# Four batches' attention weights per group: two turned by 32x32 block transposes and quadrant moves, two by TensorE

## The chip, the cores and the metric

The kernel runs on one core of one Trainium2 chip. The metric is device time in microseconds (us) of one execution. Engines are called PE (TensorE; PEld is its weight load), DVE (VectorE), ACT (ScalarE), POOL (GpSimd) and SP (the engine that issues the DMAs here).

## The reference, cut to what matters

A stack of four graph layers on x of shape (32 batches, 256 nodes, 128 features), each followed by `layernorm(x + layer(x))`: a gated graph layer, a two-layer graph network with batch norm over all 32 batches, a graph attention, and two graph convolutions followed by LSTMs over windows of 1 to 4 nodes. The change lies in the attention:

```python
Wh = jnp.einsum('bnf,fo->bno', h, W)
e = s1[:, :, None] + s2[:, None, :]
e = jnp.where(e >= 0, e, ALPHA * e)
e = jnp.where(adj_matrix[None] == 0, -jnp.inf, e)
attention = jax.nn.softmax(e, axis=-1)
h_prime = jnp.einsum('bij,bjo->bio', attention, Wh)
```

A product on PE contracts over partitions. The exponentials are made with node i on the partitions, and the mix over j needs them with j there: each batch's 256x256 matrix has to be turned, as four squares of 128x128.

## The kernel before, in words

The 32 batches are worked on in 8 groups of four (`GB = 4`). The first two layers run over all groups, because the batch norm needs all of them. Then come slots, s = 2 to 10: slot s does the attention of group s (part A, s up to 7), the graph convolutions of group s-1 (B), the LSTM of group s-2 (L) and the last norm of group s-3 (T). Groups 0 and 1 have their attention ahead of the slots. Every engine has its own program, written out by hand in `slot(...)`; engines meet by semaphores. So slots 2 to 7 do the work that the change touches, and slots 3 to 7 hold all four parts.

The LSTM has 11 steps k = 0 to 10 (`STEPS`; windows of 3 nodes are steps 4 to 6, windows of 4 are steps 7 to 10). A step is: on PE the products with x (`lstm_x`, L855, written x(k)) and with the state before (`lstm_h`, L867, written h(k)), on ACT the gates (L1231), on DVE the cell (`inner(k)`: L1712, L1718, L1722), on ACT its tanh (L1267), on DVE the state (`state(k)`, L1740), which h(k+1) waits for through `h_ok`. x(7) also waits for state(6), since the windows of 4 read what the windows of 3 have written.

The attention of a group in its slot: DVE adds the mask and takes the maximum into `MS` (`a_max`), ACT makes leaky ReLU (`a_lin`, L1184) and exponential (`a_exps`, L1194) into `E1`; PE turns each batch by four transposes into a PSUM bank (`a_turn_e`, L770), DVE copies the bank into `MS` (`a_weights`, L1640, 512 columns); PE mixes (`a_mix`, L791), ACT copies the result (L1172), PE projects it (L801), DVE adds it (L1664). The banks are `AB[0..3]`: the first half of PB, the first of PA, the second of PB, the second of PA. `a_hidden` (L1700, DVE) reads PA into the state buffer of the LSTM's next group and ends with `h1_ok`; the odd batches' bank is in PA and so waits for it.

`MS` and `E1` are the parts k = 0 and 1 of `late`, 2048 columns each. POOL does the reciprocal roots of the norms (L450), the norms' outputs (`scale2`, L518, into X1, and `tail`, L531, into the output buffer). SP only stores outputs during the slots (L425). The order on PE near the change is

```python
x(7)
x(8)
a_turn_e(s, range(GB)) if A else None
h(8)
x(9)
if A:
    a_mix(s, (0, 1, 2))
    a_project_mix(s, (0, 1))
h(9)
```

Of the kernel before, what the change touches and what calls it, by code (L numbers as in the profile page):

```python
# [100 lines left out]
def build(nc, x, xt, adj, early_in, later_in, lstm_w, out):  # L101
    ctx = ExitStack()
    with ctx:
# [20 lines left out]
        ZF = late[:, 3, 2 * BANK:4 * BANK]  # L124

# [126 lines left out]
        copied_ok = sem("copied_ok")  # L252
# [144 lines left out]
        def _(sp):  # L397
# [25 lines left out]
            for g in range(GROUPS - 1):  # L423
                sp.wait_ge(ln[3]["out"], TILES * (g + 1))
                sp.dma_start(out[g], OUT[:, g % 2]).then_inc(sent[g % 2], 16)  # L425
# [11 lines left out]
        def _(pool):  # L437
# [125 lines left out]
        def _(pe):  # L563
# [192 lines left out]
            def a_turn_e(g, some):  # L756
                f = front(g)
                for b in some:
                    if b % 2 == 0:
# [6 lines left out]
                    pe.wait_ge(exps_ok, GB * g + b + 1)  # L766
                    for c in range(NC):
                        for m in range(NC):
                            at = m * NODES + c * P
                            mm = pe.transpose(f.AB[b][:, at:at + P], f.E1[:, 2 * b + c, m * P:(m + 1) * P], ident[:])  # L770
                    mm.then_inc(et_ps, 1)
# [13 lines left out]
            def a_mix(g, some):  # L785
                pe.wait_ge(ln[1]["out"], TILES * (g + 1))
                f = front(g)
                for b in some:
                    pe.wait_ge(pt_ok, GB * (g - 1) + b + 1)
                    for m in range(NC):  # L790
                        mm = pe.matmul(f.AB[b][:, 0:NODES], turned(X2, m, b), f.MS[:, 2 * b + m, :],  # L791
# [127 lines left out]
            def slot(s, par, A, B, L, T):  # L919
# [69 lines left out]
                a_turn_e(s, range(GB)) if A else None  # L989
# [69 lines left out]
        def _(act):  # L1059
# [209 lines left out]
            def slot(s, par, A, B, L, T):  # L1269
# [102 lines left out]
        def _(dve):  # L1372
# [457 lines left out]
            def slot(s, par, A, B, L, T):  # L1830
# [48 lines left out]
                cell(6)  # L1879
                a_hidden(s - 1, 1 - par) if B else None  # L1880
# [105 lines left out]
```

## Time and profile before

| what | before |
|---|---|
| median of 3 runs | 635.05 us (634.25 to 636.53) |
| the profiled execution: its own time | 635.21 us |
| its span in the trace | 633.4 us |
| busy share PE / PEld / DVE / ACT / POOL | 98% / 68% / 74% / 69% / 26% |
| a slot with all four parts | 57.5 us |

The span is what the trace covers; the 1.8 us between it and the execution's own time lie around the program. A group of equal instructions in the timeline has one line: start, length, engine, line of code, operation, output and input, how many, and in brackets the idle time ahead of it with what ended it. For products in float32 the trace has two records each, for transposes one.

### The profile page before, as it was taken

The page shows a single profiled execution, that of the slowest core. Times are in us where ns is not written, and L with a number is a line of the kernel's source. Part 1 is how long each engine was busy: PE and PEld are TensorE (multiplying, and loading weights), DVE is VectorE, ACT ScalarE, POOL GpSimd, SP SyncE. Part 2 cuts the span into 40 slices and gives each one's busy share as a digit, 9 for nine tenths or more (in the row PEclk, how much of TensorE's full clock was granted, in tenths as well). Part 3 has the DMA queues.
Part 4 walks back from the last instruction along what each step waited for, and adds up shares of the span by engine and source line. Part 5 has one row for each costly group of instructions (what it writes and reads, how often), then busy time and mean ns, then how long its engine had stood idle before and what let it go on. Part 6 is the DMA issues. An engine that isn't in the chain of part 4 may idle for free.

```text
span 633.4 us, 9530 instructions
## 1 busy us (share of the span) xinstructions
PE 617.9 (98%) x2738; PEld 433.9 (68%) x2738; DVE 470.4 (74%) x1623; ACT 435.6 (69%) x1000; POOL 167.3 (26%) x228
## 2 busy tenths in 40 slices
PE   9999999999999999999999999999999999999994
PEld 6645556448975686578568757865885686577794
DVE  3999999877847658866887787688769867365656
ACT  3678786957847765784777678567857766546774
POOL 1465541005332003204403240340143032103201
PEclk9999999999999999999999999999999999999998
DMA  8334000000000000000000000000000000000000
GB/s 331 136 130 167 1 2 0 0 1 2 1 1 1 1 2 0 2 1 34 2 1 1 33 2 1 35 2 1 1 33 2 0 35 1 1 0 35 1 35 35
DMA packets 4372, 16.85 MB, mean 27 GB/s; under 512 B 480, under 2 KB 480, under 8 KB 4192
## 3 DMA queue, kind: packets, MB, share of 16 engines
q1 hardware_dynamic: 4320, 16.25, 6.7%
q8 instruction: 22, 0.36, 0.2%
q14 instruction: 30, 0.25, 0.1%
HBM read 12.05 MB, written 4.19 MB: 26 GB/s over the span
## 4 chain that ended last, share of the span: by engine, by line
PE 77%; DVE 3%; ACT 3%; issue 2%; POOL 1%; ACTq 0%; POOLq 0%; DVEq 0%
PE QQ L855 26%; PE QQ L867 15%; PE PA L838 4%; PE PA L810 4%; PE PB L829 2%; PE PB L820 2%; PE PB L691 2%; PE PA L691 2%; PE PA L791 2%; PE PB L791 2%; PE PA L644 1%; PE QQ L889 1%; PE PB L908 1%; PE PB L770 1%; PE PA L770 1%
## 5 line engine op out<-in xcount | busy, mean ns | idle before, releaser
L1231 ACT ACTIVATE raw<-QQ,BL 128x256 f32<-128x256 f32 (+2 forms) x279 | 150.1, 558 | 75.1 <-PE QQ L867 37.7
L855 PE MATMUL QQ<-HT,WT 128*128 128x256 f32 (+2 forms) x558 | 183.9, 474 | 1.1 <-ACT raw L1231 0.6
L450 POOL TENSOR_TENSOR RSD<-VAR,pw 128x4 f32<-128x4 f32 (+1 forms) x43 | 61.8, 1438 | 376.2 <-DVE VAR L1454 376.2
L855 PEld LDWEIGHTS QQ<-HT,WT 128*128 128x128 f32 x558 | 103.5, 190 | 59.3 <-issue 28.3
L867 PE MATMUL QQ<-HB,WT 128*128 128x256 f32 (+2 forms) x336 | 100.2, 441 | 0.4 <-DVE HB L1740 0.2
L867 PEld LDWEIGHTS QQ<-HB,WT 128*128 128x128 f32 x336 | 61.2, 190 | 29.3 <-issue 13.4
L1267 ACT ACTIVATE raw<-raw 128x256 f32<-128x256 f32 (+4 forms) x79 | 37.1, 470 | 25.9 <-DVE raw L1722 19.7
L1712 DVE SCALAR_TENSOR_TENSOR raw<-raw 128x256 f32<-128x256 f32 (+2 forms) x60 | 32.5, 542 | 20.2 <-ACT raw L1231 19.6
L1740 DVE SCALAR_TENSOR_TENSOR HB<-raw 128x256 f32<-128x256 f32 (+4 forms) x42 | 20.1, 478 | 23.5 <-ACT raw L1267 23.5
L1066 ACT ACTIVATE X<-Z,OFF,RSD 128x128 f32<-128x128 f32 x80 | 31.8, 481 | 2.5 <-POOL OFF L456 2.5
L518 POOL TENSOR_SCALAR X<-four,MEAN,RSD 128x128 f32<-128x128 f32 x64 | 30.7, 494 | 1.6
L1194 ACT ACTIVATE HB<-HB,EB 128x256 f32<-128x256 f32 x64 | 30.9, 501 | 0.2
L644 PE MATMUL PA<-AHT,X 128*128 128x256 f32 x128 | 29.6, 384 | 1.3 <-ACT X L1066 1.3
L810 PE MATMUL PA<-AD,X 128*128 128x256 f32 x128 | 30.3, 379 | 0.0
L531 POOL TENSOR_SCALAR four<-HB,MEAN,RSD 128x128 f32<-128x128 f32 x56 | 29.6, 543 | 0.7
L658 PE MATMUL QQ<-one_b,later 128*128 128x512 f32 x64 | 29.1, 597 | 0.6 <-ACT one_b L1100 0.6
L838 PE MATMUL PA<-AD,Y 128*128 128x256 f32 x128 | 29.2, 380 | 0.0
L644 PEld LDWEIGHTS PA<-AHT,X 128*128 128x128 f32 x128 | 23.7, 190 | 7.7 <-issue 4.8
L810 PEld LDWEIGHTS PA<-AD,X 128*128 128x128 f32 x128 | 23.8, 191 | 6.8 <-issue 4.1
L838 PEld LDWEIGHTS PA<-AD,Y 128*128 128x128 f32 x128 | 24.2, 190 | 4.3
L621 PE MATMUL PB<-four,AD 128*128 128x512 f32 x56 | 26.2, 611 | 0.0
L1112 ACT ACTIVATE HB<-QQ 128x512 f32<-128x512 f32 x32 | 18.0, 587 | 11.5 <-PE QQ L658 10.1
(254 smaller groups left out, 1164.5 us busy)
## 6 DMA issues: line engine op xcount, KB each, us to landing
four<-in_x SPq DMA_DIRECT2D x8, 512.0 KB, 4.0
raw<-in_xt SPq DMA_DIRECT2D x8, 512.0 KB, 6.6
out<-four SPq DMA_DIRECT2D x7, 512.0 KB, 2.7
WT<-in_lstm SPq DMA_DIRECT2D x1, 2048.0 KB, 9.3
later<-in_later SPq DMA_DIRECT2D x1, 725.5 KB, 10.2
AD<-in_adj SPq DMA_DIRECT2D x2, 256.0 KB, 4.8
out<-four SPq DMA_DIRECT2D x2, 256.0 KB, 2.0
early<-in_early SPq DMA_DIRECT2D x1, 289.0 KB, 4.7
```

The source lines that it names most:

```text
L450: pool.tensor_tensor(RSD[kk][:, ts], VAR[kk][:, ts], pw[:, ts], ALU.pow).then_inc(ln[k]["rstd"], some)
L518: pool.tensor_scalar(tile_of(X1, g, c, b), nth(f.Z2, t), MEAN[f.kk2][:, t:t + 1], RSD[f.kk2][:, t:t + 1], ALU.add, ALU.mult).then_inc(ln[2 ...
L644: mm = pe.matmul(PA[:, b * NODES:(b + 1) * NODES], tile_of(X1, g, m, b), AHT[:, m, :], start=(m == 0), stop=(m == NC - 1))
L810: mm = pe.matmul(PA[:, b * NODES:(b + 1) * NODES], tile_of(X1, g, m, b), ADJT[:, m, :], start=(m == 0), stop=(m == NC - 1))
L838: mm = pe.matmul(PA[:, b * NODES:(b + 1) * NODES], turned(Y, m, b), ADJT[:, m, :], start=(m == 0), stop=(m == NC - 1))
L855: mm = pe.matmul(steps_view(Q[q], k), WT[:, 0, (p - 1) * 4 + q, :], ht_view(par, k), start=True, stop=(s == 0))
L867: pe.matmul(Q[q][:, 0:nw * GB], WT[:, 1, (p - 1) * 4 + q, :], HS[:, (k - 1) % 2, 0:nw * GB], start=False, stop=True).then_inc(g_ps, 1)
L1066: act.activation(nth(to, t), nth(z, t), ACT.Identity, bias=OFF[kk][:, t:t + 1], scale=RSD[kk][:, t:t + 1]).then_inc(ln[k]["out"], 1)
L1194: e = act.activation(f.E1[:, t], f.E1[:, t], ACT.Exp, bias=f.EB[:, t:t + 1], scale=1.0, accum_out=DEN[:, t:t + 1] if g > 1 else None)
L1231: act.activation(TG[q][:, at:n], Q[q][:, at:n], ACT.Tanh, scale=0.5 if q == G else 0.25, bias=BL[:, p - 1, q:q + 1]).then_inc(g_ok, 1)
L1267: act.activation(TC[:, at:n], CELL[:, at:n], ACT.Tanh, scale=0.5).then_inc(tc_ok, 1)
L1712: dve.scalar_tensor_tensor(out=target[:, 0:n], in0=TG[I][:, 0:n], scalar=1.0, in1=TG[G][:, 0:n], op0=ALU.add, op1=ALU.mult).then_inc(cell_ ...
```

## The change

In slots 2 to 7 (groups g of 2 and more):

- Batches 0 and 1 are no longer turned by PE. DVE transposes every 32x32 block of a batch in place of its quadrant (`a_turn_blocks`, one instruction of 512 columns per batch, `E1` to `MS`); the blocks then stand in the right order within 32 partitions but in the wrong quadrant of 32 partitions. Sixteen moves of 32 partitions by 256 columns, for both batches at once, bring them from `MS` back to `E1`: eight by DMAs from SP (`move_blocks`), eight by copies of POOL (`carry_blocks`), each of which waits until the one before is complete, the four that stay in their quadrant among them.
- Batches 2 and 3 are turned by PE into the first and the second half of PB, and copied to `MS` as before. They wait for `y1_ok` alone, not for `h1_ok`.
- `a_mix` of batches 0 and 1 reads the moved blocks, with an access of 2x4 runs of 32 columns; it waits for all moves. Odd batches wait for `h1_ok` there, even ones for the copies that free PB.
- `a_hidden` goes behind the copy of batch 2; DVE's block transposes stand ahead of and behind `inner(6)`; ACT makes the exponentials of batch 1 one place earlier and those of batch 2 one place later.
- On POOL the eight copies stand ahead of `tail`; on SP the eight DMAs of slot s stand ahead of the store of group s-3.

```diff
+            def move_blocks(g, h):
+                sp.wait_ge(tr_ok, 2 * (g - 1))
+                for q, c in DMA_BLOCKS:
+                    sp.dma_start(block_at(1, h, c, q), block_at(0, h, q, c)).then_inc(moved_ok, 16)
...
+            def carry_blocks(g, h):
+                pool.wait_ge(tr_ok, 2 * (g - 1))
+                pool.wait_ge(yt_ok, upto(g + 3))
+                n = len(POOL_BLOCKS) * (g - 2)
+                for k, (q, c) in enumerate(POOL_BLOCKS):
+                    reach(pool, carried_ok, n + k)
+                    pool.tensor_copy(block_at(1, h, c, q), block_at(0, h, q, c)).then_inc(carried_ok, 1)
+                pool.wait_ge(carried_ok, n + len(POOL_BLOCKS))
...
-                    pe.wait_ge(pt_ok, GB * (g - 1) + b + 1)
+                    if b < 2:
+                        pe.wait_ge(moved_ok, 16 * len(DMA_BLOCKS) * (g - 1))
+                        pe.wait_ge(carried_ok, len(POOL_BLOCKS) * (g - 1))
+                    else:
+                        pe.wait_ge(pt_ok, GB + 2 * (g - 2) + b - 1)
+                    if b % 2:
+                        reach(pe, h1_ok, 2 * g)
+                    else:
+                        pe.wait_ge(pt_ok, GB + 2 * (g - 2) + b // 2 + 1)
...
-                a_turn_e(s, range(GB)) if A else None
+                a_turn_e(s, (2, 3)) if A else None
...
+            def a_turn_blocks(g, some):
+                for b in some:
+                    dve.wait_ge(exps_ok, GB * g + b + 1)
+                    dve.wait_ge(lin_ok, GB * g + 2)
+                    dve.transpose(by_block(0, b // 2)[:, :, b % 2].rearrange("p q c m i -> p (c m) q i"),
+                                  E1[:, 2 * b:2 * b + 2].rearrange("p c (m q i) -> p (c m) q i", m=NC, q=4)).then_inc(tr_ok, 1)
...
-                cell(6)
-                a_hidden(s - 1, 1 - par) if B else None
+                a_turn_blocks(s, (0,)) if A else None
+                inner(6)
+                a_turn_blocks(s, (1,)) if A else None
+                state(6)
+                a_hidden(s - 1, 1 - par) if B and not A else None
...
-                a_weights(s, (0, 1)) if A else None
+                if A:
+                    a_weights(s, (2,))
+                    a_hidden(s - 1, 1 - par)
+                    a_weights(s, (3,))
                 cell(8)
                 if A:
-                    a_weights(s, (2, 3))
                     a_inverse(s)
```

The order on DVE in a slot, from x(7)'s predecessor to the cell of step 8. L1693 is a_biased1, L1712 to L1740 the LSTM's cell and state, L1700 a_hidden, L1640 the copy out of a PSUM bank. Before:

```order
L1693 TENSOR_TENSOR Y<-PB,later 128x1024
L1712 SCALAR_TENSOR_TENSOR raw<-raw 128x340
L1718 SCALAR_TENSOR_TENSOR raw<-raw 128x340
L1722 SCALAR_TENSOR_TENSOR raw<-raw 128x340
L1740 SCALAR_TENSOR_TENSOR HT<-raw 128x85x4
L1700 TENSOR_SCALAR HT<-PA 128x4x256
...
L1712 SCALAR_TENSOR_TENSOR raw<-raw 128x256
L1740 SCALAR_TENSOR_TENSOR HB<-raw 128x256
L1640 COPY HB<-PB 128x512
L1640 COPY HB<-PA 128x512
```

The same place in the change; L1754 is now a_biased1, L1693 the block transpose, L1773 to L1801 cell and state, L1701 the copy, L1761 a_hidden:

```order
L1754 TENSOR_TENSOR Y<-PB,later 128x1024
L1693 STREAM_TRANSPOSE HB<-HB 128x4x4x32
L1773 SCALAR_TENSOR_TENSOR raw<-raw 128x340
L1779 SCALAR_TENSOR_TENSOR raw<-raw 128x340
L1783 SCALAR_TENSOR_TENSOR raw<-raw 128x340
L1693 STREAM_TRANSPOSE HB<-HB 128x4x4x32
L1801 SCALAR_TENSOR_TENSOR HT<-raw 128x85x4
...
L1773 SCALAR_TENSOR_TENSOR raw<-raw 128x256
L1801 SCALAR_TENSOR_TENSOR HB<-raw 128x256
L1701 COPY HB<-PB 128x512
L1761 TENSOR_SCALAR HT<-PA 128x4x256
L1701 COPY HB<-PB 128x512
```

Two transposes came in ahead of state(6), a_hidden went from there to behind state(7), and two of four copies are gone.

On POOL in the same slot, the change only (L552 are the eight copies, L474 and L565 the tail, L542 scale2); before, L450 and L531 stood where L474 and L565 stand, with nothing ahead of them:

```order
L534 TENSOR_SCALAR HB<-HB,BN 128x1024
L552 COPY HB<-HB 32x256 x8
L474 TENSOR_TENSOR RSD<-VAR,pw 128x8
L565 TENSOR_SCALAR four<-HB,MEAN,RSD 128x128 x8
L474 TENSOR_TENSOR RSD<-VAR,pw 128x4
L542 TENSOR_SCALAR X<-four,MEAN,RSD 128x128 x4
```

## Rows read from the trace of the kernel before

**Rows 1.** The page: engine, busy us (share of the span), instructions.

```profile
PE 617.9 (98%) x2738; PEld 433.9 (68%) x2738; DVE 470.4 (74%) x1623; ACT 435.6 (69%) x1000; POOL 167.3 (26%) x228
```

**Rows 2.** Windows, second and last of six slots: stretch, its length, busy us (instructions).

```profile
core 0: us, PE busy (x) PEld busy (x) DVE busy (x) ACT busy (x) POOL busy (x), PEclk, DMA share, GB/s
...
223.63:281.14 57.51, 57.51 (x252) 41.44 (x250) 43.34 (x148) 40.27 (x91) 9.74 (x13) 1.00 0.00 1
...
453.64:511.14 57.50, 57.50 (x251) 41.44 (x250) 43.70 (x154) 40.39 (x91) 14.52 (x21) 1.00 0.03 10
```

**Rows 3.** Timeline of PE from x(7) of a slot on: start us, length us.

```profile
453.64 3.19 PE L855 MATMUL QQ<-HT,WT 128*128 128x256 f32 x14
456.67 0.60 PE L770 MATMUL PB<-ident,HB 128*128 128x128 f32 x4
...
458.41 1.89 PE L867 MATMUL QQ<-HB,WT 128*128 128x256 f32 x8
460.14 1.89 PE L855 MATMUL QQ<-HT,WT 128*128 128x256 f32 x8
461.87 1.03 PE L791 MATMUL PB<-HB,X 128*128 128x256 f32 x4
```

**Rows 4.** Timeline of PE's weight loads in the same stretch.

```profile
453.43 3.00 PEld L855 LDWEIGHTS QQ<-HT,WT 128*128 128x128 f32 x14
...
458.30 1.60 PEld L867 LDWEIGHTS QQ<-HB,WT 128*128 128x128 f32 x8
...
461.65 0.84 PEld L791 LDWEIGHTS PB<-HB,X 128*128 128x128 f32 x4
...
465.24 1.60 PEld L867 LDWEIGHTS QQ<-HB,WT 128*128 128x128 f32 x8
```

**Rows 5.** Timeline of DVE in the same slot, idle time ahead in brackets.

```profile
448.16 1.23 DVE L1693 TENSOR_TENSOR Y<-PB,later 128x1024 f32<-128x1024 f32 x1
449.82 0.51 DVE L1712 SCALAR_TENSOR_TENSOR raw<-raw 128x340 f32<-128x340 f32 x1 [0.44 <-ACT raw L1231]
...
452.21 0.51 DVE L1740 SCALAR_TENSOR_TENSOR HT<-raw 128x340 f32<-128x340 f32 x1 [0.68 <-ACT raw L1267]
453.90 2.02 DVE L1700 TENSOR_SCALAR HT<-PA 128x1024 f32<-128x1024 f32 x1 [1.18 <-PE PA L838]
...
457.48 0.43 DVE L1740 SCALAR_TENSOR_TENSOR HB<-raw 128x256 f32<-128x256 f32 x1 [0.55 <-ACT raw L1267]
457.82 0.68 DVE L1640 COPY HB<-PB 128x512 f32<-128x512 f32 x1
...
459.98 0.54 DVE L1712 SCALAR_TENSOR_TENSOR raw<-raw 128x256 f32<-128x256 f32 x1 [0.89 <-ACT raw L1231]
...
461.94 0.47 DVE L1740 SCALAR_TENSOR_TENSOR HB<-raw 128x256 f32<-128x256 f32 x1 [0.55 <-ACT raw L1267]
```

**Rows 6.** Timeline of DVE in slot 2, whose x(7) starts at 223.63.

```profile
225.75 0.42 DVE L1712 SCALAR_TENSOR_TENSOR raw<-raw 128x256 f32<-128x256 f32 x1
226.99 0.42 DVE L1740 SCALAR_TENSOR_TENSOR HB<-raw 128x256 f32<-128x256 f32 x1 [0.82 <-ACT raw L1267]
```

**Rows 7.** Timeline of POOL in the slot of rows 3, and one wait for itself.

```profile
428.70 0.20 POOL L456 TENSOR_TENSOR OFF<-MEAN,RSD 128x8 f32<-128x8 f32 x1 [0.17 <-POOL RSD L450]
456.67 1.75 POOL L450 TENSOR_TENSOR RSD<-VAR,pw 128x8 f32<-128x8 f32 x1 [27.77 <-DVE VAR L1454]
458.52 4.21 POOL L531 TENSOR_SCALAR four<-HB,MEAN,RSD 128x128 f32<-128x128 f32 x8
471.02 1.01 POOL L450 TENSOR_TENSOR RSD<-VAR,pw 128x4 f32<-128x4 f32 x1 [8.29 <-DVE VAR L1454]
```

**Rows 8.** Groups of POOL by shape: busy us, mean ns of one.

```profile
L518 POOL TENSOR_SCALAR X<-four,MEAN,RSD 128x128 f32<-128x128 f32 x64 | 30.7, 494 | 1.6
...
L510 POOL TENSOR_SCALAR HB<-HB,BN 128x1024 f32<-128x1024 f32 x7 | 8.6, 1239 | 1.2 <-DVE HB L1578 1.2
```

**Rows 9.** SP's issues at the start of the program: start us, length us.

```profile
1.15 0.42 SPq L402 DMA_DIRECT2D four<-in_x  x1
1.62 0.42 SPq L406 DMA_DIRECT2D early<-in_early  x1
```

**Rows 10.** The page's DMA issues: count, KB each, median us from issue to landing.

```profile
raw<-in_xt SPq DMA_DIRECT2D x8, 512.0 KB, 6.6
...
out<-four SPq DMA_DIRECT2D x2, 256.0 KB, 2.0
```

More of the change, by code:

```diff
@@ L124, in build, with by_block, block_at @@
         ZF = late[:, 3, 2 * BANK:4 * BANK]
+        def by_block(k, h):
+            return late[:, k, h * COLS:(h + 1) * COLS].rearrange("p (q b c m i) -> p q b c m i", q=4, b=2, c=NC, m=NC)
+        def block_at(k, h, quadrant, slot):
+            at = h * COLS + slot * NODES
+            return late[32 * quadrant:32 * quadrant + 32, k, at:at + NODES]
+        DMA_BLOCKS = [(q, (q + n) % 4) for n in (1, 2) for q in range(4)]
+        POOL_BLOCKS = [(q, (q + n) % 4) for n in (0, 3) for q in range(4)]
         AN = late[:, 0, 0:BANK].rearrange("p (c n) -> p c n", c=NC)
@@ L251, in build @@
                              "turned_ok"))
-        copied_ok = sem("copied_ok")
+        copied_ok, tr_ok = sem("copied_ok"), sem("tr_ok")
+        moved_ok = sem("moved_ok")
+        carried_ok = sem("carried_ok")
         f_half, cf_half, cell_half, tc_half = (sem(n) for n in ("f_half", "cf_half", "cell_half", "tc_half"))
@@ L421, in _ @@
             sp.dma_start(WT[:], lstm_w).then_inc(lstm_in, 16)
-            for g in range(GROUPS - 1):
-                sp.wait_ge(ln[3]["out"], TILES * (g + 1))
-                sp.dma_start(out[g], OUT[:, g % 2]).then_inc(sent[g % 2], 16)
+            def move_blocks(g, h):
+                sp.wait_ge(tr_ok, 2 * (g - 1))
+                for q, c in DMA_BLOCKS:
+                    sp.dma_start(block_at(1, h, c, q), block_at(0, h, q, c)).then_inc(moved_ok, 16)
+            for s in range(2, GROUPS + 2):
+                if s < GROUPS:
+                    move_blocks(s, 0)
+                if s >= 3:
+                    g = s - 3
+                    sp.wait_ge(ln[3]["out"], TILES * (g + 1))
+                    sp.dma_start(out[g], OUT[:, g % 2]).then_inc(sent[g % 2], 16)
             half = TILES // 2 * P
@@ L537, in slot @@
                     scaled(s + 2)
+                if A:
+                    carry_blocks(s, 0)
                 if T:
@@ L758, in a_turn_e @@
                 for b in some:
-                    if b % 2 == 0:
+                    if g > 1:
+                        reach(pe, y1_ok, 2 * g)
+                    elif b % 2 == 0:
                         pe.wait_ge(max_ok, TILES * g + 4 * (b // 2 + 1))
@@ L766, in a_turn_e @@
                     pe.wait_ge(exps_ok, GB * g + b + 1)
+                    to = f.AB[b] if g < 2 else PB[:, b % 2 * BANK:(b % 2 + 1) * BANK]
                     for c in range(NC):
@@ L769, in a_turn_e @@
                             at = m * NODES + c * P
-                            mm = pe.transpose(f.AB[b][:, at:at + P], f.E1[:, 2 * b + c, m * P:(m + 1) * P], ident[:])
+                            mm = pe.transpose(to[:, at:at + P], f.E1[:, 2 * b + c, m * P:(m + 1) * P], ident[:])
                     mm.then_inc(et_ps, 1)
@@ L1179, in a_lin @@
                     act.wait_ge(max_ok, TILES * g + 2 * b + 2)
-                    reach(act, et_ps, GB * before(g))
+                    reach(act, et_ps, GB * before(g)) if g <= 2 else act.wait_ge(px_ps, GB * (g - 2))
                     for c in range(NC):
@@ L1303, in slot @@
                     a_lin(s, (1,))
-                    a_exps(s, (0,))
-                    a_lin(s, (2,))
+                    a_exps(s, (0, 1))
                 gates(6)
-                a_lin(s, (3,)) if A else None
+                a_lin(s, (2,)) if A else None
                 state(6)
-                a_exps(s, (1, 2)) if A else None
+                if A:
+                    a_lin(s, (3,))
+                    a_exps(s, (2,))
                 gates(7)
@@ L1638, in a_weights @@
                 for b in some:
-                    dve.wait_ge(et_ps, GB * g + b + 1)
-                    dve.tensor_copy(f.MS[:, 2 * b:2 * b + 2].rearrange("p m n -> p (m n)"), f.AB[b]).then_inc(pt_ok, 1)
+                    dve.wait_ge(et_ps, GB * g + b + 1 if g < 2 else GB * 2 + 2 * (g - 2) + b - 1)
+                    src = f.AB[b] if g < 2 else PB[:, b % 2 * BANK:(b % 2 + 1) * BANK]
+                    dve.tensor_copy(f.MS[:, 2 * b:2 * b + 2].rearrange("p m n -> p (m n)"), src).then_inc(pt_ok, 1)
             def a_sum2(g, some):
```

7 lines of the change are left out of this document (6 added, 1 removed).

## Prediction, on record before the changed kernel ran

> **What bounds the kernel now.** I read the busy times first [rows 1]: PE is busy for 98% of the span, DVE for 74%, ACT for 69%, POOL for 26%. The windows say it more sharply [rows 2]: cut from one slot's x(7) to the next one's, PE is busy for 57.51 of 57.51 us, and for 57.50 of 57.50 us in the last full slot. PE has no gap, so in these slots every microsecond taken from PE shortens the program, as long as nobody becomes late for PE. Nothing else can shorten it, so the gain cannot exceed the PE work removed. The timelines [rows 3 to 7] then tell how early each partner is.
>
> A PE product waits ahead of its weight load, so deadlines are read from the weight loads [rows 4]: x(7) at 453.43, h(8) at 458.30, the first mix at 461.65, h(9) at 465.24.
>
> **The change part by part.**
>
> *Transposes leave PE.* Between 456.67 and 458.41 the sixteen transposes of four batches run [rows 3]: 1.74 us, half of it 0.87 us per slot. Six slots (2 to 7) give 5.2 us. The mixes of batches 0 and 1 now stream eight runs of 32 columns instead of one of 256. I cost that at nothing: x(7) to x(10) already read the state buffer in runs of 4 columns, and x(9) takes exactly the 1.73 us (460.14 to 461.87) that h(8), which reads a contiguous buffer, takes (458.41 to 460.14) [rows 3].
>
> *DVE: two block transposes in, two copies out.* No row shows a block transpose. The nearest one is a one-input instruction over as many columns, the copy out of a bank, 0.68 us [rows 5], and I take that. Below lies the cell operation with 340 columns, 0.51; above, a_hidden, which writes strided and takes 2.02 us for 1024 columns, so 1.01 for 512 [rows 5]. The total on DVE is then unchanged; the place counts. The first transpose goes into the gap of 0.44 us ahead of inner(6), the second into the gap of 0.68 us ahead of state(6) [rows 5], where DVE waits for ACT. With T = 0.68 state(6) comes 0.24 + 0 = 0.24 us later. It ended at 452.72, and x(7)'s weights load at 453.43: a margin of 0.71, which covers it. The cover is gone when 2T - 1.12 = 0.71, at T = 0.92. At T = 1.01 PE waits 0.19 us per slot, 1.1 us in all.
>
> *h(8) is asked for 0.87 us earlier.* It waits for state(7), which ended at 457.91, while h(8)'s weights now want to load at 458.30 - 0.87 = 457.43. What helps is that a_hidden has left its place ahead of inner(7): in slot 2, where no last norm delays DVE and DVE is in time for ACT, state(7) starts at 226.99 and ends at 227.41 [rows 6], 3.78 us behind x(7). In the slot of rows 3 that is 457.42. ACT then sets the time (three exponential instructions' worth of work stand between the gates and the tanh, as before). 457.42 against 457.43 is no margin: with the semaphore's way and a weight load that no longer hides, I take 0.1 us of waiting per slot, 0.6 us in all. Lower end: 0. Upper end: POOL now works during this stretch, and beside POOL's tail DVE's cell operation took 0.54 instead of 0.42 us and its state 0.47 [rows 5, 6]; with that on both, 0.3 per slot, 1.8 us.
>
> *a_hidden moves behind state(7)* and one copy. From 457.5: copy to 458.1, a_hidden to 460.0, second copy to 460.6. Queued behind are inner(8) and state(8). The chain from inner(8) to the end of state(8) took from 459.98 to 462.41 [rows 5], so 2.43 us; it now ends at 463.0, and h(9)'s weights load at 465.24 - 0.87 = 464.37. Covered, with 1.3 us left. The odd mix that waits for `h1_ok` comes after 461.
>
> *The moves.* Both block transposes are done at about 451.5 + 0.24 + 0.68 = 452.4. The first mix's weights load at 461.65 - 0.87 = 460.8. So there are 8.4 us for the moves.
> SP: issues follow one another by 0.47 us [rows 9], the eighth starts 3.3 us after the first; landing 2.0 us for the smallest store, 6.6 us for the slowest kind of load [rows 10]. I take 2.0, since a move is 32 KB and touches no DRAM: done at 457.7. At 6.6 it would be 462.3, 1.5 us late.
> POOL: 128 columns take 0.49 us and 1024 take 1.24 [rows 8], so 0.84 ns per column more and 0.60 us for 256; the wait for its own result adds 0.17 [rows 7]. Eight in a row: 6.2 us, done at 458.6, 2.2 us early. Lower end: 0.49 each with no wait, 3.9 us. Upper end: 1.24 + 0.17 each, 11.3 us, done at 463.7.
> Behind the copies stands the tail, 1.75 + 4.21 us [rows 7]: done at 464.6; POOL's next work comes at 471.02 - 0.87. Covered. On SP only the store stands behind.
>
> *ACT* swaps exponentials of batches 1 and 2 between two places of equal length; nothing.
>
> **Sum.** 635.21 (the profiled execution) - 5.2 + 0.6 = 630.6. The median of the runs lies 0.16 below that execution, so 630.4 us.
>
> **Two rules of the Trainium skill.** Beside POOL's tail DVE's two-input cell operation lengthened by 0.12 us, from 0.42 to 0.54 [rows 5, 6]: a small brush, not a blockade. "SBUF — State Buffer", section "Who interferes with whom", says that a DVE instruction with two SBUF inputs and a POOL instruction that reads SBUF exclude each other for a whole instruction, and the loser fully blocks. By that rule the result would be rival B's; this trace agrees that there is an interaction but not with its size.
> The nearest row for a block transpose is 0.68 us. "VectorE: DVE Perf Modes", section "The three transpose paths", gives 311 ns for 128x128 in bf16; four of them would be 1.24 us (an estimate from that page), and the sum by it would be about 634; no row here shows it.
>
> **The rivals.**
>
> *A. The copies on POOL are late (slower).* Place: the wait of the first mix for `carried_ok`. If a copy that shifts quadrants costs as much as POOL's costliest one-input row, 1.24 + 0.17, the eight end at 463.7, 2.9 us behind 460.8; less the 0.87 saved this is 2.0 us per slot, 12 us: 647. It decides from (8.4 + 0.87)/8 = 1.16 us per copy on; from 1.05 on it eats into the gain. For it: only 32 of 128 partitions work, the copy leaves its quadrant, and nothing like it is in the trace. Against it: all elementwise rows of POOL lie below 0.6 us at this size. The DMAs at 6.6 us would do the same at a lower price (1.5 us late, 0.6 net per slot, 639).
>
> *B. The gain is given back on DVE (no change).* Two ways to the same time. A block transpose of twice the copy, 1.36 us, makes state(6) late by 2.72 - 1.12 - 0.71 = 0.89 us per slot, 5.3 us: 635. Or a copy of POOL (0.60) stands in the way of state(6) and of state(7) each once a slot: 0.24 + 0.60 - 0.71 = 0.13 and 0.1 + 0.60 = 0.7, together 0.8 per slot, with the 5.2 saved 634.8. For: both new partners of DVE are unseen. Against: the 0.12 us above.
>
> *C. Half a gain:* T between 0.9 and 1.2, or 0.3 to 0.5 us of waiting at h(8): 631.9 to 633.5.
>
> *D. The full gain,* nothing waits: 629.9. It lies within the forecast's own range.
>
> That the change doesn't do what it says I exclude: the order of instructions shows the transposes gone.
>
> **How the numbers follow.** Forecast with D: 0.66 (629.4 to 631.9). C: 0.13. B: 0.11. A: 0.10. The range 629.4 to 634.0 holds forecast, C and a part of B, and leaves out A and the rest of B. A measurement of this kernel can tell 0.3%, 1.9 us, from no change, so faster means below 633.1: forecast and nearly all of C, 0.78; same: B with a crumb of C, 0.12; slower: A, 0.10.
>
> **What the changed profile would show.** Right: transposes on PE down by 48 and slots of 56.7 us in the windows; PE idle ahead of L867's h(8) of 0 to 0.3 us per slot and nowhere else; block transposes of about 0.7 us; POOL's copies about 0.6 us with 0.1 to 0.2 between; the first mix not waiting. Wrong, if PE or its weight load waits for POOL or a DMA at the mix (A), for state(6) at x(7) or for a much later state(7) at h(8) (B, C), or if the mixes of batches 0 and 1 last longer than 0.87 us for two.

## The result, and the profile after

| what | before | changed |
|---|---|---|
| median | 634.97 us (634.25 to 636.53, 4 runs) | 630.85 us (630.61 to 631.24, 4 runs) |
| the profiled execution: its own time / span | 635.21 / 633.4 us | 631.24 / 629.2 us |
| a slot with all four parts | 57.5 us | 56.65 to 56.7 us, slot 3: 57.0 us |

The ratio is 0.9932 with an interval of [0.9913, 0.9952]. Measured once more beside the kernel before, the unaltered change gave 0.9946 [0.9929, 0.9962]. Both intervals lie below 1: the change is faster, by 0.5 to 0.7%, 4.1 us in the first pair of medians.

The page, the lines that answer to [rows 1] and the two new kinds of work:

```profile
PE 612.8 (97%) x2690; PEld 428.9 (68%) x2690; DVE 471.9 (75%) x1623; ACT 434.4 (69%) x1000; POOL 188.6 (30%) x276
...
L552 POOL COPY HB<-HB 32x256 f32<-32x256 f32 x48 | 22.3, 464 | 137.6 <-DVE HB L1693 135.0
...
HB<-HB SPq DMA_DIRECT2D x48, 32.0 KB, 1.8
```

PE has 48 records fewer (six slots of eight transposes) and 5.1 us less to do; DVE's busy time rose by 1.5 us, POOL's by 21.3. The windows, cut from x(7) to the next x(7) as in [rows 2]:

```profile
core 0: us, PE busy (x) PEld busy (x) DVE busy (x) ACT busy (x) POOL busy (x), PEclk, DMA share, GB/s
223.30:279.90 56.60, 56.60 (x244) 40.69 (x243) 43.75 (x153) 40.18 (x91) 13.77 (x22) 1.00 0.02 6
279.90:336.90 57.00, 56.84 (x243) 40.59 (x242) 44.49 (x154) 40.14 (x91) 19.14 (x31) 1.00 0.04 15
...
450.25:506.90 56.65, 56.65 (x243) 40.60 (x242) 44.07 (x154) 40.14 (x91) 17.94 (x30) 1.00 0.04 15
```

57.50 less 0.87 would be 56.63. Four of these stretches come out at 56.6 to 56.7; slot 3 is 0.35 us longer. PE from x(7) on, the place of [rows 3]: x(7), the eight transposes, h(8), x(9), the first of the mixes.

```profile
450.25 3.19 PE L906 MATMUL QQ<-HT,WT 128*128 128x256 f32 x14
453.27 1.04 PE L809 MATMUL PB<-ident,HB 128*128 128x128 f32 x8
454.14 1.94 PE L918 MATMUL QQ<-HB,WT 128*128 128x256 f32 x8
455.92 1.89 PE L906 MATMUL QQ<-HT,WT 128*128 128x256 f32 x8
457.64 1.03 PE L842 MATMUL PB<-HB,X 128*128 128x256 f32 x4
458.51 1.03 PE L842 MATMUL PA<-HB,X 128*128 128x256 f32 x4
```

h(8) stands 3.89 us behind x(7) instead of 4.77, and takes 1.78 us up to x(9) instead of 1.73: that is all PE waits for it. The mixes that read the blocks still follow one another by 0.87 us. The weight loads of x(7), h(8) and the first mix [rows 4]:

```profile
450.03 3.00 PEld L906 LDWEIGHTS QQ<-HT,WT 128*128 128x128 f32 x14
...
454.08 1.59 PEld L918 LDWEIGHTS QQ<-HB,WT 128*128 128x128 f32 x8
...
457.43 0.84 PEld L842 LDWEIGHTS PB<-HB,X 128*128 128x128 f32 x4
```

DVE in that slot [rows 5]: block transposes ahead of and behind inner(6), state(6) at 448.81, state(7) at 453.60, the copies at 453.95 and (not shown) 456.42 with a_hidden between them.

```profile
445.90 0.70 DVE L1693 STREAM_TRANSPOSE HB<-HB 128x512 f32<-128x512 f32 x1
446.53 0.47 DVE L1773 SCALAR_TENSOR_TENSOR raw<-raw 128x340 f32<-128x340 f32 x1
...
448.05 0.70 DVE L1693 STREAM_TRANSPOSE HB<-HB 128x512 f32<-128x512 f32 x1
448.81 0.52 DVE L1801 SCALAR_TENSOR_TENSOR HT<-raw 128x340 f32<-128x340 f32 x1
...
451.82 0.43 DVE L1773 SCALAR_TENSOR_TENSOR raw<-raw 128x256 f32<-128x256 f32 x1 [1.27 <-ACT raw L1282]
453.60 0.43 DVE L1801 SCALAR_TENSOR_TENSOR HB<-raw 128x256 f32<-128x256 f32 x1 [1.36 <-ACT raw L1318]
453.95 0.68 DVE L1701 COPY HB<-PB 128x512 f32<-128x512 f32 x1
454.55 2.01 DVE L1761 TENSOR_SCALAR HT<-PA 128x1024 f32<-128x1024 f32 x1
```

Counted from x(7), state(6) starts at -1.44 us; before it was -1.43 [rows 3, 5]. The first block transpose makes inner(6) 0.11 us late (1.77 us behind a_biased1, before 1.66), and the way from inner(6) to state(6) is as much shorter (2.28 instead of 2.39 us). POOL's copies and tail, and SP's issues:

```profile
448.81 4.14 POOL L552 COPY HB<-HB 32x256 f32<-32x256 f32 x8 [23.31 <-DVE HB L1693]
...
454.78 4.04 POOL L565 TENSOR_SCALAR four<-HB,MEAN,RSD 128x128 f32<-128x128 f32 x8
```

One of the eight copies in a narrower view. It starts 0.12 us behind inner(7) (451.82, 0.43 us long) and takes 0.56 us, where the median of all 48 is 0.40:

```profile
451.94 0.56 POOL L552 COPY HB<-HB 32x256 f32<-32x256 f32 x1
```

SP:

```profile
448.78 4.95 SPq L441 DMA_DIRECT2D HB<-HB  x8
```

The copies end at 452.95, 4.5 us before the first mix's weight load. The issues are 0.62 us apart, so the last one starts at 453.1 and lands 1.8 us later, at 454.9: 2.5 us to spare.

**Where the time went.** The span fell by 4.2 us. The transposes gave 5.22 (six times 0.87). Ahead of the x(7) of slot 2 0.33 us was gained (223.30 against 223.63); by what was not traced. Back went 0.25 at h(8), and three single delays of 0.35 us: -5.22 - 0.33 + 0.25 + 1.05 = -4.25. The first of the three is in slot 3, where the state of step 10 comes late and with it the chain of states up to the one that PE waits for at x(2):

```profile
300.88 0.42 DVE L1801 SCALAR_TENSOR_TENSOR HT<-raw 128x256 f32<-128x256 f32 x1 [0.90 <-ACT raw L1318]
```

```profile
306.74 2.84 PE L906 MATMUL QQ<-HT,WT 128*128 128x512 f32 x6 [0.16 <-DVE HT L1801]
```

The bracket is 0.55 at this step in the other slots, with tanh equally early; DVE paused for 0.35 us with its input ready. The second is ahead of a_hidden in slot 8 ([2.05] where the kernel before had [1.70]), the third at a state instruction of the last slot at 606.50 ([0.83] among neighbours of [0.48]).

### The profile page after: what moved, and what is told of

It is laid out like the page before. It is cut to its first block, busy times and chain, and to the rows that moved or that the text cites. A ratio compares the mean times of both kernels' runs of the same rounds, so it can differ in the third digit from the quotient of the medians.

```text
span 629.2 us, 9560 instructions
## 1 busy us (share of the span) xinstructions
PE 612.8 (97%) x2690; PEld 428.9 (68%) x2690; DVE 471.9 (75%) x1623; ACT 434.4 (69%) x1000; POOL 188.6 (30%) x276
## 4 chain that ended last, share of the span: by engine, by line
PE 75%; DVE 4%; ACT 3%; issue 2%; POOL 1%; ACTq 0%; POOLq 0%; DVEq 0%
PE QQ L906 26%; PE QQ L918 15%; PE PA L889 4%; PE PA L861 4%; PE PB L880 2%; PE PB L871 2%; PE PB L727 2%; PE PA L727 2%; PE PA L842 2%; PE PB L842 2%; PE PA L680 1%; PE PB L809 1%; PE PB L959 1%; PE QQ L694 1%; PE PA L852 1%
## 5 line engine op out<-in xcount | busy, mean ns | idle before, releaser
L474 POOL TENSOR_TENSOR RSD<-VAR,pw 128x4 f32<-128x4 f32 (+1 forms) x43 | 61.3, 1426 | 213.3 <-DVE VAR L1506 212.9
L552 POOL COPY HB<-HB 32x256 f32<-32x256 f32 x48 | 22.3, 464 | 137.6 <-DVE HB L1693 135.0
L1773 DVE SCALAR_TENSOR_TENSOR raw<-raw 128x256 f32<-128x256 f32 (+2 forms) x60 | 32.7, 545 | 20.4 <-ACT raw L1282 19.7
L1801 DVE SCALAR_TENSOR_TENSOR HB<-raw 128x256 f32<-128x256 f32 (+4 forms) x42 | 19.9, 474 | 28.1 <-ACT raw L1318 28.1
L542 POOL TENSOR_SCALAR X<-four,MEAN,RSD 128x128 f32<-128x128 f32 x64 | 31.0, 498 | 1.6
L565 POOL TENSOR_SCALAR four<-HB,MEAN,RSD 128x128 f32<-128x128 f32 x56 | 28.8, 530 | 0.7
```

Of the source, the lines that this page charges most:

```text
L474: pool.tensor_tensor(RSD[kk][:, ts], VAR[kk][:, ts], pw[:, ts], ALU.pow).then_inc(ln[k]["rstd"], some)
L542: pool.tensor_scalar(tile_of(X1, g, c, b), nth(f.Z2, t), MEAN[f.kk2][:, t:t + 1], RSD[f.kk2][:, t:t + 1], ALU.add, ALU.mult).then_inc(ln[2 ...
L1773: dve.scalar_tensor_tensor(out=target[:, 0:n], in0=TG[I][:, 0:n], scalar=1.0, in1=TG[G][:, 0:n], op0=ALU.add, op1=ALU.mult).then_inc(cell_ ...
```

## The experiments

Slots are measured from x(7) to x(7), places in a slot from its x(7). Each kernel is the changed one with the edit shown. The kernel before gave 634.46 us beside the first four, 634.64 beside the next four, 634.54 beside the two with all four batches turned by blocks and 634.84 beside the last one; times of different groups are compared by their ratio to it.

**What do the moves cost?** Both block transposes, the DMAs and POOL's copies are left out.

```diff
-                    move_blocks(s, 0)
...
-                    carry_blocks(s, 0)
...
-                        pe.wait_ge(moved_ok, 16 * len(DMA_BLOCKS) * (g - 1))
-                        pe.wait_ge(carried_ok, len(POOL_BLOCKS) * (g - 1))
+                        pe.wait_ge(exps_ok, GB * g + 2)
...
-                a_turn_blocks(s, (0,)) if A else None
                 inner(6)
-                a_turn_blocks(s, (1,)) if A else None
```

> This kernel leaves out the block transposes on DVE, the eight DMAs and the eight copies of POOL, so batches 0 and 1 of groups 2 to 7 are mixed with exponentials that are not turned. Theory (transposes and moves are hidden, the PE time alone counts): 630.3 to 631.0 us, as the changed kernel, h(8) still waiting some 0.05 us per slot. Rival (the moves slow DVE or PE by contention and cost the missing microsecond): 629.3 to 629.9 us.

Measured: 630.06 us (629.94 to 630.26), ratio 0.9931 [0.9916, 0.9945], slots of 56.76. The ratio of the full change, 0.9932 and 0.9946, has an interval that overlaps it in both measurements: the new work on three engines costs nothing that can be measured. Its median is 0.8 us lower all the same, but of the three delays of 0.35 us that the change pays this kernel has two less: a_hidden of slot 8 has [1.70] again, no state of the last slot stands out, and one delay is new, at state(7) of slot 2 (slot 2 takes 57.03 us). h(8) starts at +3.93 here and takes 1.83 us, 0.1 us a slot worse than with the moves in. With no copies ahead of it, POOL's tail (eight instructions from 451.69 to 455.5) now runs beside state(7), which takes 0.52 instead of 0.43 us in slots 3 to 7:

```profile
453.37 0.52 DVE L1796 SCALAR_TENSOR_TENSOR HB<-raw 128x256 f32<-128x256 f32 x1 [1.36 <-ACT raw L1313]
```

**Was it needed to move a_hidden?** It goes back to its old place ahead of inner(7).

```diff
-                a_hidden(s - 1, 1 - par) if B and not A else None
+                a_hidden(s - 1, 1 - par) if B else None
...
                     a_weights(s, (2,))
-                    a_hidden(s - 1, 1 - par)
                     a_weights(s, (3,))
```

> a_hidden back ahead of state(7), all else as changed. Theory (h(8) hangs on state(7), and state(7) on a_hidden's place): in slots 3 to 7 state(7) ends 4.27 us behind x(7) as before the change, h(8)'s weights want to load at 3.83, so PE waits about 0.45 us per slot, 2.2 to 2.6 us in all: 633.0 to 633.5 us. Rival (the place of a_hidden is indifferent, PE's saving alone counts): 630.5 to 631.2 us.

Measured: 634.09 us (633.65 to 635.26), ratio 0.9995 [0.9986, 1.0004]. The change is undone. PE in the same slot:

```profile
452.09 3.19 PE L906 MATMUL QQ<-HT,WT 128*128 128x256 f32 x14
455.11 1.04 PE L809 MATMUL PB<-ident,HB 128*128 128x128 f32 x8
456.61 1.99 PE L918 MATMUL QQ<-HB,WT 128*128 128x256 f32 x8 [0.47 <-DVE HB L1801]
```

h(8) starts at +4.52 instead of +3.89 and slots take 57.36 us. Slot 2, where the norm of part T is missing, keeps +3.89. The mechanism was as expected, its size was not: 0.69 us per slot, of which I had foreseen 0.45. 0.2 of the rest comes from POOL: of the small instructions of the norm between a_hidden and inner(7), the second starts beside the last of POOL's copies and takes 0.38 us in slots 3 to 7, where the kernel before has 0.17, and state(7) starts at +4.04 instead of +3.84 as before:

```profile
454.26 0.38 DVE L1497 TENSOR_TENSOR DIF<-STL 128x8 f32<-128x8 f32 x1
```

Without this one reordering, PE would have had 0.87 us less to do per slot and would have waited nearly as long.

**How much room have the moves?** All sixteen by DMA, then all sixteen by POOL.

```diff
-        DMA_BLOCKS = [(q, (q + n) % 4) for n in (1, 2) for q in range(4)]
+        DMA_BLOCKS = [(q, (q + n) % 4) for n in (1, 2, 0, 3) for q in range(4)]
...
-                    carry_blocks(s, 0)
...
-                        pe.wait_ge(carried_ok, len(POOL_BLOCKS) * (g - 1))
```

> All sixteen blocks by DMAs of SP. Theory (issues follow each other by 0.62 us and the mix waits for the last landing): 15 x 0.62 + 1.8 = 11.1 us behind the transposes' end at 448.8, so 459.9 against the 457.4 at which the first mix's weights load; 2.5 us per slot, 15 us: 645 to 647 us. Rival (issues and landings overlap elsewhere, the deadline is later than read): under 635 us.

Measured: 654.06 us (653.3 to 656.41), ratio 1.0315 [1.0294, 1.0336]: 23 us more than the change, where I had expected 15. Sixteen issues take 10.0 us and the first mix starts at +9.9 to +10.2 (slot 2: +11.0) instead of +7.4, 2.5 us late. That part was right. But slots 2 to 6 last 59.2 to 62.1 us, up to 5.4 more than in the change. In one of the long ones, PE from x(9) to the third mix, and the granted clock:

```profile
413.09 1.89 PE L903 MATMUL QQ<-HT,WT 128*128 128x256 f32 x8
417.50 1.10 PE L839 MATMUL PB<-HB,X 128*128 128x256 f32 x4 [2.53 <-issue]
418.44 1.59 PE L839 MATMUL PA<-HB,X 128*128 128x256 f32 x4
419.82 1.91 PE L839 MATMUL PB<-HB,X 128*128 128x256 f32 x4
```

```profile
core 0: us, PE busy (x) PEld busy (x) DVE busy (x) ACT busy (x) POOL busy (x), PEclk, DMA share, GB/s
...
417.00:420.00 3.00, 2.50 (x9) 2.12 (x10) 0.00 (x0) 0.38 (x1) 0.00 (x0) 0.79 0.46 182
420.00:425.00 5.00, 5.00 (x24) 4.37 (x23) 1.81 (x6) 2.39 (x6) 0.00 (x0) 0.78 0.00 0
425.00:430.00 5.00, 5.00 (x28) 4.41 (x27) 3.23 (x16) 2.71 (x7) 1.48 (x3) 1.00 0.00 2
```

After 2.53 us without a product the same four products take 1.91 instead of 1.03 us: part of the stretch ran at the lower of the clock's two levels (1.2 GHz against 2.4), and this slot lost 1.8 us more than the 2.8 by which its mix was late. The clock fell in five of the six slots, after waits of 3.48, 2.26, 2.23, 2.53 and 2.27 us at this place. In slot 6 PE waited 2.21 us, the clock stayed at 1.00, and the slot lost only the wait (59.2 us). A late partner of PE thus cost 1.5 to 1.9 times its lateness where the clock fell. No wait of the change comes near these.

```diff
-        POOL_BLOCKS = [(q, (q + n) % 4) for n in (0, 3) for q in range(4)]
+        POOL_BLOCKS = [(q, (q + n) % 4) for n in (1, 2, 0, 3) for q in range(4)]
...
-                    move_blocks(s, 0)
...
-                        pe.wait_ge(moved_ok, 16 * len(DMA_BLOCKS) * (g - 1))
```

> All sixteen blocks by copies of POOL. Theory (a copy is 0.40 us, up to 0.76 beside DVE, 0.52 from one to the next on average, and 8.6 us are free): 8.3 us, done 0.3 us ahead of the mix, 630.5 to 632 us. Rival (beside DVE's busier second half copies take 0.76 us): done at about 459, 1.6 us late per slot, about 640 us.

Measured: 631.45 us (630.83 to 632.62), ratio 0.9954 [0.9938, 0.9971]. The first mix starts at +7.50 us and does not wait: sixteen copies take 7.86 us, 449.18 to 457.04. POOL alone would do; the DMAs save it 3.7 us per slot that nobody needs. Slots take 56.79 us, 0.14 more than in the change, again with h(8) at +3.94 and 1.83 us long. Here it is the copies that stand beside state(7): it starts 0.13 us behind one of them (453.83, 0.39 us long) and takes 0.53 us.

```profile
453.96 0.53 DVE L1798 SCALAR_TENSOR_TENSOR HB<-raw 128x256 f32<-128x256 f32 x1 [1.36 <-ACT raw L1315]
```

**What margin has state(6)?** A second block transpose ahead of each, into a buffer that nobody reads.

```diff
+                    dve.transpose(one_c[:, b * BANK:(b + 1) * BANK] ...).then_inc(junk_ok, 1)
                     dve.transpose(by_block(0, b // 2)[:, :, b % 2] ...).then_inc(tr_ok, 1)
```

> Each of the two block transposes of a slot is preceded by one more, whose result goes to a buffer that nobody reads: their cost on DVE is doubled, nothing else changes. By the trace of the changed kernel a block transpose takes 0.70 us and its successor starts 0.6 to 0.63 us after it; the margin of state(6) before x(7)'s weight load is 0.7 us. Prediction's formula (2T - 1.12 - 0.71 with T = 1.26 for a pair): PE waits 0.7 us per slot at x(7), 4.2 us in all, ratio to the kernel before 1.000. My theory after the profile: the pair shares the gap with ACT's wait, so 0.3 to 0.5 us per slot, 1.8 to 3 us, 632.5 to 634. Rival (DVE has slack there throughout, the position of the block transposes does not matter): 631, ratio 0.993.

Measured: 631.02 us (630.52 to 632.73), ratio 0.9947 [0.9932, 0.9962]; the change beside it gave 631.01. The time is the rival's. state(6) and the weight load of x(7):

```profile
449.88 0.47 DVE L1805 SCALAR_TENSOR_TENSOR HT<-raw 128x340 f32<-128x340 f32 x1
```

```profile
450.41 2.89 PEld L907 LDWEIGHTS QQ<-HT,WT 128*128 128x128 f32 x14 [0.29 <-DVE HT L1805]
```

state(6) starts 0.53 us ahead of x(7) instead of 1.44, yet a slot takes 56.74 us instead of 56.65: state(6) is 1.0 us later, PE 0.1. So DVE has no slack throughout, as the rival had it, but nearly as much as the second pair takes. The weight load is held up by 0.3 us. In the change it starts 0.22 us ahead of its product (450.03 and 450.25), here together with it (both 450.41), 0.06 us behind the end of state(6). So the deadline was later than the start of the weight load by which I read it.

**Do the three pauses belong to DVE's instruction stream?** In the program of the change they stand at places 960, 1856 and 1984 of DVE's instructions, waits counted: 7 and 1 times 128 apart. The unaltered change was run again, and with 32 and 64 one-element writes on DVE ahead of the slots.

```diff
+            dve.memset(GZ[:, 0:1, 0:1], 0.0)
...
             slots(slot)
```

> The changed kernel unaltered, as the reference beside the next three on the same chip. Both theories: 630.9 us, ratio 0.993 (0.991 to 0.996). If DVE's three pauses of 0.35 us depend on the place in the instruction stream and not on chance, they stand in the same three places as in the changed kernel's first profile: slot 3 takes 57.0 us from x(7) to x(7) and the others 56.6 to 56.7.

> Thirty-two one-element writes on DVE ahead of the slots (they cost some 2 to 3 us there at most, perhaps hidden), so that every later instruction of DVE stands 32 places further on. Theory (a pause of some 0.35 us every 128 instructions of DVE, by position in its stream, mostly hidden): slot 3's pause in state(10) is gone, so slot 3 takes 56.7 instead of 57.0 us; the pause of slot 8 ahead of a_hidden is gone; new ones can show at the state instructions at 253.9 (slot 2), 362.7 (slot 4), 499.3 (slot 6) and at 596.0 (lanes). Rival (the pauses belong to those slots, for example to what other engines do there): slot 3 still 57.0, slot 8 still late by 0.35 us.

> The same with sixty-four writes. Theory: the pause is missing at the places named for the changed kernel; new ones can show at the instructions that stood at 247 (slot 2), 277 (slot 3, cell), 382 (slot 5), 423 (slot 5), 459.4 (slot 6), 587.5 (lanes). Rival: slot 3 still takes 57.0 us and slot 8 is still late by 0.35 us.

Measured: 631.01 us (631.0 to 631.73) for the change, 630.58 (630.41 to 630.77) with 32 and 630.18 (629.77 to 630.22) with 64 instructions more. Slots 2 to 6 from x(7) to x(7) take 56.59, 57.03, 56.59, 56.68, 56.68 us in the change, 56.59, 56.69, 57.03, 56.68, 56.68 with 32 and 56.58, 56.67, 56.69, 56.68, 56.66 with 64. The state of slot 3 first in the change, then with 32, where the place at 362.7 is now the late one, with PE's wait for it:

```profile
300.99 0.42 DVE L1801 SCALAR_TENSOR_TENSOR HT<-raw 128x256 f32<-128x256 f32 x1 [0.91 <-ACT raw L1318]
```

```profile
300.42 0.43 DVE L1801 SCALAR_TENSOR_TENSOR HT<-raw 128x256 f32<-128x256 f32 x1 [0.55 <-ACT raw L1318]
...
362.57 0.69 DVE L1801 SCALAR_TENSOR_TENSOR HT<-raw 128x512 f32<-128x512 f32 x1 [0.37 <-issue]
```

```profile
363.32 2.84 PE L906 MATMUL QQ<-HT,WT 128*128 128x512 f32 x6 [0.16 <-DVE HT L1801]
```

In the last slot the pause moved as named beforehand too: with 32 to the state at 595.94 ([0.85] where its neighbours have [0.48]), with 64 to the one at 586.65 ([0.90] instead of [0.55]). a_hidden of slot 8 has [1.69] in both. The other two places named for 32 show it as well, at 254.15 in slot 2 and at 499.55 in slot 6, but PE did not wait for them and the slots are no longer than before:

```profile
254.15 0.69 DVE L1801 SCALAR_TENSOR_TENSOR HB<-raw 128x512 f32<-128x512 f32 x1 [1.12 <-ACT raw L1318]
499.55 0.51 DVE L1801 SCALAR_TENSOR_TENSOR HB<-raw 128x340 f32<-128x340 f32 x1 [1.18 <-ACT raw L1318]
```

In the unshifted change these two brackets are 0.77 and 0.83. With 64 no slot is longer. Counted as above, the late instructions stand at places 832, 1216, 1728 and 1984 with 32 and at 1984 with 64. Each of these places, like the three of the change, is 64 more than a multiple of 128. The rival is out.

The kernel before has such a pause too. The wait instruction at its place 1472, behind the state at 440.87, starts 0.39 us behind it, where the same pair has 0.04 us in the five other places it stands at; PE is busy throughout, so it cost nothing there.

**Does the idea carry to all four batches?** All four are turned by blocks, and ACT makes the exponentials of batch 3 behind the tanh of state(7).

```diff
-                a_turn_e(s, (2, 3)) if A else None
...
-                    a_mix(s, (0, 1, 2))
+                    a_mix(s, (0, 1))
                     a_project_mix(s, (0, 1))
                 h(9)
                 x(10)
-                    a_mix(s, (3,))
+                    a_mix(s, (2, 3))
...
                 gates(7)
-                a_exps(s, (3,)) if A else None
                 state(7)
+                a_exps(s, (3,)) if A else None
...
-                    a_weights(s, (2,))
+                    a_turn_blocks(s, (2, 3))
                     a_hidden(s - 1, 1 - par)
-                    a_weights(s, (3,))
...
+                    move_blocks(s, 1)
...
+                    carry_blocks(s, 1)
```

> All four batches are turned by blocks: the last eight transposes leave PE too, the exponentials of batch 3 go behind the tanh of state(7) on ACT, the second pair's moves run on SP and POOL before POOL's tail, and the mix of batch 2 goes behind x(10). PE has nothing to fill the 0.87 us between x(8) and h(8), so h(8) waits for state(7). If state(7) follows its inputs (theory), it ends about 0.35 us earlier than now, since the exponentials of batch 3 (0.98 us on ACT) no longer stand ahead of its tanh: h(8) at +3.5 us instead of +3.89 behind x(7), 0.3 to 0.4 us per slot, 2 to 2.4 us in all: 628.5 to 629.0. Rival (state(7) is set by something else, e.g. the gates): h(8) stays at +3.9, no gain, 630.9. Second rival (the second pair's moves are late for the mixes, or POOL's tail delays its next work): PE waits at a mix, slower than 631.

Measured: 626.27 us (625.87 to 626.66), ratio 0.9871 [0.9855, 0.9888], slots of 56.09. It beats both kernels, and the change by twice what I expected. In the traces 3.95 us of it lie between the first x(7) (223.3 in both) and that of slot 8, among them the pause of slot 3, which is not there; 0.85 us lie behind, and there the other two are missing as well (a_hidden of slot 8 has [1.70], the states of the last slot [0.48]). So 1.05 of the 4.8 us are pauses that this program happens to hide, and some 3.75 are the change itself. PE's x(7) and h(8), and the tanh of state(7):

```profile
447.66 3.19 PE L904 MATMUL QQ<-HT,WT 128*128 128x256 f32 x14
450.70 1.99 PE L916 MATMUL QQ<-HB,WT 128*128 128x256 f32 x8
```

```profile
449.69 0.42 ACT L1315 ACTIVATE raw<-raw 128x256 f32<-128x256 f32 x1
450.01 0.49 ACT L1242 ACTIVATE HB<-HB,EB 128x256 f32<-128x256 f32 x1
```

The tanh starts at +2.03 instead of +2.85, 0.82 us earlier, where I had reckoned with 0.35: two exponentials had held it up in full, and inner(7) never did. h(8) follows x(8) with almost no gap (+3.04). Of the 0.87 us per slot 0.58 arrive. 0.12 are left at h(8), where x(9) now starts 1.83 us behind, and 0.2 behind the mixes, where the weight load of the second projection waits 0.22 us for ACT's copy.

Two tries at the rest. First, a quarter of a_spread1 goes between x(8) and h(8):

```diff
...
-                a_spread1(s - 1) if B else None
+                a_spread1(s - 1, None, (0, 1, 2) if A else None) if B else None
                 x(7)
                 x(8)
+                a_spread1(s - 1, None, (3,)) if A and B else None
```

> As the one before, and the last quarter of a_spread1 (four products, 0.87 us) goes from ahead of x(7) into the place between x(8) and h(8). Then x(7) is asked for 0.87 us earlier and its state(6) has a margin of 0.7, so 0.2 us of waiting there; h(8) has 0.87 us more room. Theory: 0.65 to 0.75 us per slot less than the changed kernel, 4 us in all: 626.5 to 627.5. Rival (state(6) is later than I think, since the block transposes stand before it): 0.3 us per slot, 629. Second rival: the moves are late, slower than 631.

Measured: 627.20 us (627.06 to 627.36), ratio 0.9886 [0.9871, 0.99], slots of 56.29: 0.9 us slower than without it. That the time lies in the range named is luck: the range counted as the gain of the filling what the kernel without it turned out to have already. The weight loads of x(7) now wait twice:

```profile
447.31 1.16 PEld L905 LDWEIGHTS QQ<-HT,WT 128*128 128x128 f32 x6 [0.23 <-DVE HT L1800]
448.83 1.59 PEld L905 LDWEIGHTS QQ<-HT,WT 128*128 128x128 f32 x8 [0.36 <-ACT raw L1281]
```

I had seen the wait for state(6), not the one for ACT, which is still emptying x(7)'s bank of gates(6). What fills PE between x(8) and h(8) is taken from ahead of x(7), where it covered more.

Second, h(9) runs ahead of the projections of batches 0 and 1:

```diff
                     a_mix(s, (0, 1))
-                    a_project_mix(s, (0, 1))
                 h(9)
+                a_project_mix(s, (0, 1)) if A else None
                 x(10)
```

> The kernel that turns all four batches by blocks, with one change: h(9) runs ahead of the projections of batches 0 and 1. In its profile PE's weight load for the second projection waits 0.22 us for ACT's copy of the mix, once a slot, while state(8) is done 1.0 us before h(9)'s weight load. Theory (that wait is paid): 0.2 us per slot less, slots of 55.9 instead of 56.1 us, 1.2 us in all, 625.1, ratio to the kernel before 0.985. Rival (the sums of batches 0 and 1 on DVE now stand in the way of inner(9), whose state(9) comes about 1 us later and is late for h(10) or the norm behind it late for POOL): no gain or slower, 626.3 to 628.

Measured: 626.11 us (625.92 to 626.32), ratio 0.9864 [0.9847, 0.988], slots of 56.04. The 0.22 us wait is gone, and in its place is

```profile
399.88 1.59 PEld L916 LDWEIGHTS QQ<-HB,WT 128*128 128x128 f32 x8 [0.38 <-DVE HB L1798]
```

h(9) asked 0.87 us earlier, and state(8) is not ready. The time is nearer to the rival's, the reason is neither's: one wait for another. 0.04 us a slot were gained in the trace, and in the ratios no gain over the kernel without this edit (0.9871) is clear of noise.

## Why the prediction was right, point by point

630.4 us were predicted, 630.85 measured; the range held it. The mechanism was right: PE gained what left it, and nearly nobody became late. That the two numbers lie so close is in part luck: the 0.6 us put down for waits at h(8) came out at 0.25, and 1.05 us of pauses that no term held stand against 0.33 us gained ahead of the slots, which no term held either.

- *Transposes leave PE, 5.2 us.* Right: h(8) stands 0.88 us nearer to x(7), and slots are at 56.65. The mixes in runs of 32 columns cost nothing, as taken.
- *The block transpose, T = 0.68.* Measured 0.70 (0.700 to 0.705 in twelve). The page "VectorE: DVE Perf Modes" of the Trainium skill, section "The three transpose paths", would have made it 1.24, an estimate from its bf16 figure; the trace disagrees for float32 with 512 columns. The copy of the same size was the better guide.
- *state(6) 0.24 later, with a margin of 0.71.* The lateness was 0, and the margin larger: doubling the transposes made it 1.0 us late and cost 0.1 us a slot. Rival B's first way was therefore priced too high: by its formula a pair of 1.26 us in each place would make state(6) 1.40 us late and cost 0.7 us a slot. Two errors, both on the safe side. The gaps were read from the brackets, which count from the end of an instruction, though the next one can start before that end (0.62 us behind a transpose of 0.70); and behind a late inner(6) the cell operations follow each other faster. And the margin was counted to the start of the weight load: of the 0.3 us by which state(6) missed it, 0.2 were the time by which the load is early for its product.
- *h(8) asked 0.87 us earlier, 0.1 us of waiting per slot.* 0.04 measured. state(7) ended at +3.78, exactly where slot 2 of before had put it. This reading of a slot in which the disturbing instruction is missing carried the forecast: with a_hidden back in its place all of the gain was lost.
- *ACT ahead of the tanh of state(7).* Two exponentials with their sums stand between the gates and the tanh, 1.0 us, not three. Nothing in the sum hung on the count. That these two alone set the time of the tanh showed when they were moved behind it.
- *POOL beside DVE.* In the change inner(7) at 451.82 takes 0.43 us, as with the copies left out (0.42), since the copy then running has only 0.06 us left; the copy that starts behind it takes 0.56 instead of 0.40 and costs nobody anything. Where more of POOL's instruction is left, DVE's pays. "SBUF — State Buffer" of the Trainium skill, section "Who interferes with whom", lets a two-input DVE instruction and a POOL instruction that reads SBUF exclude each other. The traces agree: a cell or state instruction that starts while one of POOL's has 0.20, 0.25, 0.27, 0.31 or 0.35 us left takes 0.04, 0.10, 0.12, 0.16 or 0.20 us longer: it is held until POOL's is over, less 0.15 us. Only beside instructions of POOL that were lengthened themselves (over 0.6 us left) DVE's were not. The 0.12 us that the prediction took for a small brush [rows 5, 6] were such a wait (POOL's instruction ran 0.27 us on), and its judgement that the size speaks against the rule does not hold. Rival B's second way is real, but a copy of 0.40 us can cost at most 0.25 by this, not 0.60, and in the change it does not meet state(6) or state(7).
- *POOL's copies, 0.60 + 0.17.* 0.52 from one to the next, 0.40 long; done at +2.70 instead of +4.96. The argument that all elementwise rows of POOL lie below 0.6 us overlooked L450, 1.75 us for 8 columns [rows 7]; a copy turned out to be cheaper than any of them. *SP, 0.47 apart and 2.0 to land.* 0.62 and 1.8, done at +4.65 instead of +4.06; still 2.5 us early. Rival A's condition (1.16 us per copy) was far off.
- *a_hidden moves behind state(7).* Covered, as said: h(9) does not wait.
- *What the sum left out.* Three pauses of DVE, 1.05 us, nearly all of the difference between 629.9 (rival D) plus 0.25 and what came, against 0.33 us that were gained ahead of the slots. In the kernel before PE waited nowhere in the slots, so a pause like the one at its place 1472 was hidden. A kernel whose partners have little margin left pays for them.

## What to carry to other kernels

When PE loses work, ask for each product behind the gap what it was hiding; here one instruction moved out of the way of state(7) was worth over 3 us, most of the gain. The best price for a wait without a neighbour is an instance of the same place without it (slot 2 here), and a deadline is the product's start, not the start of its weight load (at x(7) 0.2 us later). Work that waits on a recurrence between engines belongs behind the step of the recurrence, not ahead: two exponentials moved by one place on ACT brought state(7) 0.8 us forward, and that let the removal of the other eight transposes pay.

## What the runs showed of the hardware that was not expected

- DVE pauses for about 0.35 us at fixed places of its program, whatever stands there. All places named here are 64 more than a multiple of 128, waits counted: 960, 1856 and 1984 in the change, 832, 1216, 1728 and 1984 with 32 instructions put ahead, 1984 with 64, 1472 in the kernel before. The 32 or 64 idle instructions changed the time by -0.4 and -0.8 us, 0.2 and 0.3 of that ahead of the x(7) of slot 2. What DVE does in the pause was not shown.
- Waits of 2.23 to 3.48 us on PE were followed by products at almost half speed (1.91 us for 1.03) in five slots, one of 2.21 us was not. The mean granted clock of that kernel was 0.984, and those slots lost 1.5 to 1.9 times the lateness.
- A DVE instruction with two inputs in SBUF that starts while one of POOL's runs lengthens by what is left of that one, less 0.15 us (0.04 us for 0.20 left, 0.20 for 0.35, in five traces), unless POOL's was lengthened itself. A copy of POOL that starts 0.12 us behind a cell instruction takes 0.56 instead of 0.40 us.
- A copy on POOL from one quadrant of 32 partitions to another takes 0.40 us for 256 columns, less than a scaling of 128 columns on 128 partitions (0.49 [rows 8]).
